# Self attention in a decoder chain: turned weights in two 64-row halves, masks in quarters, projection behind the scores, rotation and inversion later

## The reference, cut

```python
q = einsum('bsm,hmd->bshd', resid, W_Q) + b_Q        # k, v likewise
q = _apply_rotary(q, sin, cos, ROT_DIM)              # k likewise
k = concatenate([k, broadcast(virtual_k)], axis=1)   # v likewise: 128 + 16
scores = einsum('bqhd,bkhd->bhqk', q, k) / SCALE
mask = arange(kv_len)[None, :] <= arange(s)[:, None] + VKV
pattern = softmax(where(mask, scores, -inf))
z = einsum('bhqk,bkhr->bqhr', pattern, v_g)          # 8 values a head
out = einsum('bqhd,hdm->bqm', z, W_O)
```

## Time and profile before

| | |
|---|---|
| median of 3 executions | 3583.1 us (3573.9 to 3586.54) |
| the profiled execution | 3583.83 us, of which the span is 3582.0 us |
| mean granted clock of TensorE | 0.883 of full speed |
| busy over the span | PE 78%, PEld 56%, DVE 69%, ACT 55%, POOL 43% |
| stage `l0_attn`, 92 to 730 us | 638.00 us: PE 586.80 busy, DVE 516.65, ACT 449.71, POOL 310.77 |

### The profile page before, as it was taken

One profiled execution on the slowest core, in us unless ns is written; L12 is line 12 of the kernel. 1 busy time (PEld: TensorE's weight loads), 2 busy tenths in 40 slices (PEclk: granted clock), 3 DMA queues, 4 the chain that ended last, 5 costly groups with the idle time before them and its releaser, 6 DMA issues. The chain is left out here.

```text
span 3582.0 us, 77843 instructions
## 1 busy us (share of the span) xinstructions
PE 2797.2 (78%) x28859; PEld 2018.7 (56%) x28859; DVE 2465.0 (69%) x7100; ACT 1969.0 (55%) x3803; POOL 1541.9 (43%) x1205
## 2 busy tenths in 40 slices
PE   2899999987865867989899999966655656868956
PEld 1677777655555755656455555544433446845646
DVE  6688888856555876967666676649992553568955
ACT  2577777644444754755555555545532734556747
POOL 3554555412247723520255555523221248815544
PEclk9999999999967987999999999977768858979958
DMA  4333333212102301000000000000007012300013
GB/s 136 55 54 56 56 55 53 45 59 97 49 23 66 89 27 66 2 1 1 1 2 2 2 2 2 3 1 18 19 27 217 12 41 66 95 27 20 2 32 99
DMA packets 103267, 150.94 MB, mean 42 GB/s; under 512 B 26266, under 2 KB 76524, under 8 KB 101756
## 3 DMA queue, kind: packets, MB, share of 16 engines
q1 hardware_dynamic: 91546, 123.11, 13.8%
q0 software_dynamic: 10912, 22.70, 1.9%
q10 hardware_dynamic: 434, 0.15, 0.0%
HBM read 81.13 MB, written 49.04 MB: 36 GB/s over the span
## 5 line engine op out<-in xcount | busy, mean ns | idle before, releaser
L458 DVE TENSOR_REDUCE MX<-banks 128x8 f32<-128x1152 f32 x128 | 173.1, 1352 | 102.1 <-PE banks L275 101.9
L2450 POOL TENSOR_TENSOR SM<-SM,RZ 128x1232 f32<-128x1232 f32 x64 | 143.8, 2248 | 194.0 <-DVE RZ L2492 192.9
L1727 POOL DMA_INDIRECT expert_results<-Y,DST x181 | 177.1, 979 | 82.0 <-issue 34.3
L1714 POOL DMA_INDIRECT sorted_rows<-SRC,IDX x160 | 156.7, 979 | 128.8 <-DVE IDX L1843 82.2
L427 POOL TENSOR_TENSOR KT<-KT,FL 128x512 f32<-128x512 f32 x64 | 81.6, 1275 | 302.6 <-DVE FL L447 302.6
L1496 PE MATMUL banks<-XC,WR 128*128 128x128 f32 x1448 | 196.7, 280 | 0.2 <-ACT XC L1616 0.2
L384 ACT COPY PT<-banks 128x384 f32<-128x384 f32 x384 | 170.3, 478 | 47.2 <-PE banks L285 43.4
L2434 ACT COPY PT<-banks 77x512 f32<-77x512 f32 x256 | 143.0, 583 | 87.1 <-PE banks L2353 84.4
L285 PE MATMUL banks<-sb_c_ident,SM 128*128 128x128 f32 x1152 | 182.6, 286 | 10.1 <-ACT PT L384 9.6
L1496 PEld LDWEIGHTS banks<-XC,WR 128*128 128x128 f32 x1448 | 179.9, 195 | 2.9 <-ACT XC L1616 2.1
L2779 POOL TENSOR_TENSOR KQ<-T,EX 128x1024 f32<-128x1024 f32 x32 | 75.9, 2372 | 235.6 <-ACT EX L2760 235.6
(11 more groups left out here) (565 smaller groups left out, 8604.8 us busy)
## 6 DMA issues: line engine op xcount, KB each, us to landing
FL<-RAW SPq DMA_DIRECT2D x512, 64.0 KB, 2.3
sorted_rows<-in_zeros_dram SPq DMA_DIRECT2D x33, 528.0 KB, 8.6
XR<-sorted_rows SPq DMA_DIRECT2D x181, 66.0 KB, 1.9
SRC<-expert_results SPq DMA_DIRECT2D x16, 512.0 KB, 7.8
T<-s4d_k_dram SPq DMA_DIRECT2D x8, 1024.0 KB, 10.3
weight_region<-in_l_ffn__wall_dram SPq DMA_DIRECT2D x1, 4112.0 KB
film_dram<-F SPq DMA_DIRECT2D x8, 512.0 KB, 2.9
FO<-film_dram SPq DMA_DIRECT2D x8, 512.0 KB, 5.1
```

The costliest lines, as they stand in the source:

```text
L458: nc.vector.tensor_reduce(MX[:, n % 2], sc, AXX, ALU.max).then_inc(s.mx, 1)
L1714: nc.gpsimd.indirect_dma_start(out=rows, out_offset=bass.IndirectOffsetOnAxis(ap=IDX[:, k, t:t + 1], axis=0), in_=SRC[:, t, k, :], in_offs ...
L1727: nc.gpsimd.indirect_dma_start(out=results, out_offset=bass.IndirectOffsetOnAxis(ap=DST[:, j % ST:j % ST + 1], axis=0), in_=Y[:, j % ST, : ...
L2450: nc.gpsimd.tensor_tensor(SM[:, t % 3], SM[:, t % 3], bc(RZ[:, t % 2, :].unsqueeze(2), [P, H, L]), ALU.mult).then_inc(s.nm, 1)
```

## The change

The turned weights now come as halves. Each of the eight head slices is turned by two products, one for its 64 upper and one for its 64 lower rows (64 rows by 128 columns of weights, 64 columns moving); the upper half lands in bank 4, the lower in bank 5, through the view `turned`. The slice of the virtual keys is turned whole, into bank 7. ACT copies them with two copies in place of three: 1024 columns and 128 columns.

Each mask is made by two products of 64x64 weights into the two halves of a bank's partitions, so a step has eight of 288 columns; `MASK` and the constant `f_causal` grow to two versions.

All of T now stands ahead of the masks. Its waits are the exponential, the copies of the step before, the second item of the step before taken out of bank 7 or 4 (ahead of the virtual keys' slice: the first item), and at every fourth step the residual, since the projection now uses bank 5. The projection stands behind the scores, and the items and it wait for both copies.

z has one bank (6) in place of two. So the mix of an even step, which begins a new z, waits for `normalise` of that very step; `normalise` moves up on DVE, from the step's end to right behind the maximum; `invert` moves on ACT from the end of the odd step to the even step behind the copies. Last, the sine product of step 6 moves to step 7 and that of step 0 to step 1.

```diff
-        MASK = ctx.enter_context(nc.sbuf_tensor(f"maskb_{nc.next_id()}", [P, 2, K], BF16))
+        MASK = ctx.enter_context(nc.sbuf_tensor(f"maskb_{nc.next_id()}", [P, 2, 2, K], BF16))
...
+        HALF = (slice(0, 64), slice(64, 128))
...
+        def bank_of(item, p):
+            if p == 0:
+                return PS[:, 4 + FIRST.index(item) % 2, :]
+            return PS[:, 4 if [row for row in TAKE if item in row][0].index(item) else 7, :]
...
+        turned = PS[:, 4:6, :].rearrange("p r (h q) -> p h r q", q=64)
+        turned_vk = PS[:, 7, 0:P]
+
+        z_bank = PS[:, 6, 0:2 * P].rearrange("p (r q) -> p r q", r=2)
...
-            return PS[:, 0, 384:384 + P]
+            return PS[:, 5, 0:P]
...
-                    if n >= 2 * NR and n % NR == 0:
-                        project(n // NR - 2)
                     for i in range(4):
                         if i == 2 and n >= 1:
                             pe.wait_ge(s.sub, n)
-                        nc.tensor.matmul(PS[:, i, 0:2 * K], IDB[:], MASK[:].rearrange("p a k -> p (a k)"), start=True, stop=False)
+                        at = HALF[i % 2]
+                        for late in range(2):
+                            nc.tensor.matmul(PS[HALF[late], i, 0:2 * K], IDB[at, at], MASK[at, late].rearrange("p a k -> p (a k)"), start=True, stop=False)
...
-                def weights_T(n, c):
-                    item = f"T{c}"
-                    if c == 0:
-                        pe.wait_ge(s.ex, n + 1)
-                    ring_free(pe, item, n)
-                    for q in range(3):
-                        ins = nc.tensor.transpose(ring(item, n)[:, q * P:(q + 1) * P], SM[:, n % 3, 3 * c + q, :], E.ident)
+                def weights_T(n):
+                    pe.wait_ge(s.ex, n + 1)
+                    if n >= 1:
+                        pe.wait_ge(s.pt, 2 * n)
+                    if n + 1 >= 2 * NR and (n + 1) % NR == 0:
+                        pe.wait_ge(s.res, (n + 1) // NR - 1)
+                    new = due(n + 1) if n >= 1 else [(item, 0) for item in FIRST] + due(0) + due(1)
+                    for item, p in new[1:]:
+                        taken(pe, item, p)
+                    for k in range(8):
+                        for r in range(2):
+                            ins = nc.tensor.transpose(turned[:, k, r, :], SM[HALF[r], n % 3, 1 + k, :], E.ident[HALF[r], HALF[r]])
                     ins.then_inc(s.pt_ps, 1)
+                    for item, p in new[:1]:
+                        taken(pe, item, p)
+                    nc.tensor.transpose(turned_vk, SM[:, n % 3, 0, :], E.ident).then_inc(s.pt_ps, 1)
...
-                    z = z_of(m)[:, r % 2]
-                    pe.wait_ge(s.pt, 3 * n + 2 + a)
+                    z = z_bank[:, r % 2]
                     if a == 0:
+                        pe.wait_ge(s.pt, 2 * n + 2)
                         if n % NPR == 0:
                             pe.wait_ge(s.v, p + 1)
-                        if n % 2 == 0 and m >= 2:
-                            pe.wait_ge(s.zt, m - 1)
+                        if n % 2 == 0 and m >= 1:
+                            pe.wait_ge(s.zt, m)
...
-                        weights_T(n - 2, 0)
-                        weights_T(n - 2, 1)
+                        weights_T(n - 2)
                     if n < N:
                         scores(n)
-                    elif n % NR == 0:
-                        pe.wait_ge(s.sub, N)
+                    if live:
+                        pe.wait_ge(s.pt, 2 * (n - 2) + 2)
+                    elif n < 2:
+                        taken(pe, FIRST[-1], 0)
+                    if n >= 2 * NR and n % NR == 0:
                         project(n // NR - 2)
-                    if live:
-                        weights_T(n - 2, 2)
...
-                def weights(k):
-                    n, c = k // 3, k % 3
-                    act.wait_ge(s.pt_ps, k + 1)
-                    if c == 0 and n >= 2:
+                def weights(n):
+                    act.wait_ge(s.pt_ps, 2 * n + 1)
+                    if n >= 2:
                         act.wait_ge(s.z_ps, n - 1)
-                    nc.scalar.copy(PT[:, n % 2, 3 * c:3 * c + 3, :].rearrange("p h q -> p (h q)"), ring(f"T{c}", n)[:, 0:3 * P]).then_inc(s.pt, 1)
+                    nc.scalar.copy(PT[:, n % 2, 1:9, :].rearrange("p h (r q) -> p h r q", r=2), turned).then_inc(s.pt, 1)
+                    act.wait_ge(s.pt_ps, 2 * n + 2)
+                    nc.scalar.copy(PT[:, n % 2, 0, :], turned_vk).then_inc(s.pt, 1)
...
-                        weights(3 * (n - 2))
-                        weights(3 * (n - 2) + 1)
+                        weights(n - 2)
+                    if n >= 4 and n % 2 == 0 and (n - 4) // 2 < HALVES:
+                        invert((n - 4) // 2)
                     if 1 <= n <= N:
                         act.wait_ge(s.sub, n)
                         nc.scalar.activation(SM[:, (n - 1) % 3], SM[:, (n - 1) % 3], ACT.Exp, scale=SCALE).then_inc(s.ex, 1)
-                    if live:
-                        weights(3 * (n - 2) + 2)
                     for item, p in due(n):
                         take(item, p)
-                    if n >= 3 and n % 2 == 1 and (n - 3) // 2 < HALVES:
-                        invert((n - 3) // 2)
...
+                    if n >= 4 and n % 2 == 0:
+                        normalise((n - 4) // 2)
                     dve.wait_ge(s.mx, n + 1)
                     if n >= 3:
-                        dve.wait_ge(s.pt_ps, 3 * (n - 2))
+                        dve.wait_ge(s.pt_ps, 2 * (n - 2))
...
-                    if n >= 4 and n % 2 == 0 and (n - 4) // 2 < HALVES:
+                    if n >= N and n % 2 == 0 and (n - 4) // 2 < HALVES:
                         normalise((n - 4) // 2)
                     if n >= 3 and n % 2 == 1 and (n - 3) // 2 < HALVES:
                         spread((n - 3) // 2)
-                    if n // NPR + 1 < NP and n % NPR in (3, 5, 6):
-                        turn(NR * (n // NPR + 1) + (3, 5, 6).index(n % NPR))
-                    if n >= NPR and n // NPR < NP and n % NPR == 0:
+                    if n // NPR + 1 < NP and n % NPR in (3, 5, 7):
+                        turn(NR * (n // NPR + 1) + (3, 5, 7).index(n % NPR))
+                    if n >= NPR and n // NPR < NP and n % NPR == 1:
...
-    c["f_causal"] = np.where(np.arange(P + 16)[None] <= p + 16, 0, -1e30).astype(f)
+    c["f_causal"] = np.where(np.arange(P + 16)[None, None] <= p[:, :, None] % 64 + 64 * np.arange(2)[None, :, None] + 16, 0, -1e30).astype(f)
```

46 lines of the change are left out of this document (16 added, 30 removed).

## The result

The changed kernel takes 3640.1 us (median of 4 executions, 3636.8 to 3642.1) against 3583.2 (4 executions), a ratio of 1.0162, 95% interval 1.0142 to 1.0183: 57 us slower, where 25 were forecast. The direction and most of the mechanisms held, the size did not.

A forecast was written before the change was run, and what follows sets the result against it. TensorE was taken to bound most steps, VectorE odd steps with one item. Longer steps, 2.26 us per 16 steps, gave 17 us and the clock 7: 24 us on 3583.8, forecast 3608, range 3578 to 3642.

The forecast's parts named there:

- What bounds: In the touched stage TensorE sets most steps, VectorE odd ones with one item; 16 steps take 81.06 us against 78.8.
- the handover: From the end of normalise on VectorE to TensorE's virtual values in even steps: estimated at 0.05 us, bounded by 0.15.
- Four steps with two items: Steps 1 and 3: 4.58 us of TensorE work with items as 2 x 0.75, plus 0.30 waiting for a copy: 4.88.
- TensorE's own work: Halves, virtual slice and masks with their shape changes take 1.27 us a step instead of 1.59, 0.32 less.
- The new wait: Even steps' mix waits for normalise, closing a loop from maximum to maximum: 4.82 us, or 5.02 with the residual.
- The scalings: Four layernorm scalings behind step 7's sine product: one free, three held by GpSimd, about 3.9 us; the step 8.17.
- The rival of scalings not held: Layernorm scalings cost 1.3 to 2.66 us instead of 3.9, TensorE keeps its clock: 3581 to 3592 us; chance 0.17.
- The clock: After TensorE's idle time beside the scalings, a spell at half clock costs 1.0 us, seven times: 7 us.
- ScalarE's copies at nothing: ScalarE's two copies of turned slices are covered by TensorE's work and cost nothing; uncovered, 0.1 to 0.2 us a step.
- The sign of being wrong: In the changed profile, TensorE waiting for the copies behind the scores would show the forecast wrong; no size given.
- The sine product's transfer wait: VectorE's 2.14 us wait for eight transfers goes when step 6's product moves to step 7; no further gain counted.
- load-paced halves: Rival: pairs of halves take 0.10 us by their 128-column loads, 12 of 16 steps 0.33 longer: 3638 us; chance 0.15.

The follow-up runs named there:

- run 5: Changed kernel with layernorm statistics, root and scalings one step later, plus the eight head slices turned whole instead of as halves: 3599.1 us, ratio 1.0047.
- run 4: Changed kernel with z in two banks again, normalise at the step's end, virtual slice in z's bank, items in banks 4 and 5: 3589.2 us, ratio 1.0021.
- run 1: Changed kernel with only the four layernorm scalings moved to the end of the next, even step: 3595.2 us, ratio 1.0039.
- run 9: Kernel before with only the sine products of steps 6 and 0 moved to steps 7 and 1: 3593.5 us, ratio 1.0038.
- run 11: Changed kernel with the sine products put back at steps 6 and 0: 3631.5 us, ratio 1.0136.
- run 3: Changed kernel with 30 added mask products on TensorE at each step n % 16 = 8, ahead of the mix: 3619.8 us, ratio 1.0100.
- run 13: Changed kernel with the identity cast to bf16 ahead of the two mask casts: 3639.2 us, ratio 1.0162.
- run 6: Changed kernel with layernorm statistics, root and scalings one step later, plus each mask made by one 128x128 product: 3585.1 us, ratio 1.0010.
- run 10: Kernel before with sine products moved to steps 7 and 1 and layernorm statistics, root and scalings one step later: 3555.8 us, ratio 0.9928.

## Why the prediction was wrong, point by point

- **What bounds.** Right: TensorE by steps, VectorE in odd ones with one item. The undisturbed steps lie within 0.12 of the forecast in all 16 places. Summed they are 82.27 against 81.06: 1.2 a period, 9 us in 7.5 periods. Eight even steps are off by 0.06 to 0.09, by the handover, 0.12 instead of 0.05. Four steps with two items are off by 0.12: two items were summed as 2 x 0.75, and take 1.61 here and 1.62 in the kernel before (weight loads, first here, then before):

```profile
283.73 0.73 PEld L238 LDWEIGHTS banks<-weight_region,XT 128*128 128x128 f32 x4 [0.16 <-ACT PT L385]
...
285.34 0.41 PEld L296 LDWEIGHTS banks<-PT,sb_l_attn__vv 128*128 128x128 f32 x2
```

```profile
274.39 0.73 PEld L248 LDWEIGHTS banks<-weight_region,XT 128*128 128x128 f32 x4
...
276.01 0.41 PEld L298 LDWEIGHTS banks<-PT,sb_l_attn__vv 128*128 128x128 f32 x2
```

- **TensorE's own work**, 1.27: right to the hundredth, 0.65 + 0.26 + 0.36. That whole slices would cost more was not asked in the prediction; run 5 shows 0.23 a step.
- **The new wait**: right in kind and size; run 4 shows it by taking it away. One reason in it was wrong and its number right: the weights of the first product don't load during the wait, they load at 327.31, 0.12 behind the end of `normalise`, and virtual values take 0.42 all the same.
- **The scalings**: 3.9 forecast, 4.02 measured, held for the reason given; runs 1, 9 and 11 show it. The rival of scalings not held is out.
- **The clock is the step that failed.** The term was 1.0 us in seven places, 7 us. Measured are 86.0 - 82.27 = 3.7 a period, or 26 us. Two things were wrong in it. I took the length of slow work, 3.4 us, from one stretch and discounted it by what VectorE might bound; here the clock stayed at 0.50 for 6.8 us, all of it on TensorE's path: mix, T, masks and scores take 2.1 longer there, the items behind them 0.8 (319.59 to 322.21 where two items otherwise take some 1.8), and 2.6 is what run 3 gives back a place, 20 us in all. And I counted one kind of place. The statistics leave TensorE idle too, 2.26 in each of seven places, and in three of them step 6 was long, 6.99 twice and 6.06 once, instead of 4.88: the other 6 us. The windows of one such place:

```profile
384.00:386.30 2.30, 0.12 (x1) 0.00 (x0) 2.27 (x9) 1.70 (x5) 2.30 (x3) 0.95 0.69 109
386.30:387.00 0.70, 0.62 (x2) 0.50 (x2) 0.70 (x3) 0.00 (x0) 0.70 (x1) 0.50 0.62 105
387.00:392.00 5.00, 5.00 (x59) 3.39 (x59) 1.06 (x3) 2.24 (x3) 1.56 (x2) 0.50 0.02 4
```

  In a loop without slack, 2.3 us with 0.12 busy were followed by 0.50. In the kernel before, with the statistics in the same place, TensorE idles beside them for at most 0.50 at a time and the clock stayed at 1.00; in run 4, which gives the second z back and leaves the statistics where they are, it idles for 0.71, and step 6 is 4.0 with none long. So this short hold costs the clock only with the single z; the long one of the scalings costs it with two z as well (runs 4 and 9). Why the same 2.26 cost the clock in three of seven places here, in five in run 3, in six in run 11 and in all seven in run 13 stays open.
- **ScalarE's copies at nothing**: right in effect. The sign of being wrong, TensorE waiting for them behind the scores, is there (0.15 at 325.37 above), but from the first weights of the scores to those of the item it takes 0.71 (324.66 to 325.37), where it took 0.70 before to the next work.
- **The sine product's transfer wait** went, as forecast. It comes back in run 11, and run 9 shows that without it, and with the scalings held, the kernel before would be 14 us slower.
- **The start** had no term: 3.7 us in the trace, which no total has shown.

Together: 26 (undisturbed steps, 82.27 - 78.8 by 7.5) + 26 (clock) + 4 (start) = 56 of the 57. The forecast's own sum for these was 17 + 7 + 0. In the traces the last maximum of the stage comes 55.4 us later than before, at 781.0 against 725.6. The measured time lies near the one forecast for load-paced halves, which run 5 rules out: that nearness is chance.

## What to carry to other kernels

When a resource that two iterations shared is cut to one, sum the loop that this closes, and then look for every place where some other engine is held once in a while: with no slack each of these is an idle time of TensorE, and the clock behind it can cost as much as the wait itself (26 us of clock beside 26 of longer steps here). Short SBUF-to-SBUF operations of VectorE shouldn't stand right behind the operation that releases a row of GpSimd work. The gain of a change can be real and drowned: halves and quarters were worth 21 and 8 us here (runs 5 and 6), and the version with two z and the layernorm elsewhere ran at 3540. But of its 41 us 26 are the order of VectorE's work, which the kernel before can have as well (run 10): compare a change with the best order of both kernels.
